# Expert blocks of two sizes, 512 and 256 rows, in place of 512 alone

## The chip, the cores and the metric

The kernel runs on one core of a Trainium2 chip. The metric is the device time of one execution in microseconds. The kernel before takes 2289.64 us, the median of three runs.

## What is computed

The input is 256 images of 128 channels and 7 x 7 pixels, that is 12544 tokens of 128 numbers. Six layers follow one another, each with a residual: window attention, attention over the pixels of an image with 1x1 convolutions, self-attention and a first mixture of experts, multi-scale self-attention and a second mixture of experts.

```python
def reference(x, ...):
    x = _L0_conv_ref(x, ...)
    x = _L1_conv_ref(x, ...)
    t = _to_tokens(x)
    t = t + _L2_attn_ref(_ln_t(t))
    t = t + _L2_ffn_ref(_ln_t(t), ...)
    t = t + _L3_attn_ref(_ln_t(t), ...)
    t = t + _L3_ffn_ref(_ln_t(t), ...)
    return _from_tokens(t, x)
```

Both mixtures have 8 experts, and each token goes to the two with the highest gate scores, so 25088 token-expert pairs (rows) are to be worked on in each. An expert is two matrix products with a Gelu between them, 128 to 192 to 128 numbers in the first mixture and 128 to 512 to 128 in the second:

```python
h = gelu(x @ W1[expert] + b1[expert])
y = h @ W2[expert] + b2[expert]
out = gate_1 * y_1 + gate_2 * y_2
```

## The kernel before

The program is a sequence of phases. The two that matter here are the expert stages, called moe2 and moe3 in names, and the dispatch phase ahead of each.

**Dispatch.** For each group of tokens it computes the two experts and gates, and GpSimd writes each token's row (128 numbers, and behind them its target row, its second expert and both gates; 528 bytes) to the region of its expert in `expert_rows`, in DRAM (L1558). Each expert has a region of its own of 13 x 1024 rows. When all are counted, `Dispatch.table` (L1512 to L1546, VectorE) turns the eight counts into a table of blocks: for each block its expert `blk_e`, its first row `blk_row` and the expert whose weights it takes, `blk_w`. A block is 512 rows of one expert; since a count need not be a multiple of 512, there are NBLK = 56 (L46), the most that any counts can need. Those left over point behind the last region, to a place without tokens. SyncE puts pad rows behind each expert's last token with eight stores (L1273). The constants of the table (`c_upto8`, `c_steps`, `c_blocks`) are loaded in `weights` (from L1250 on), ahead of `d_pad`, which holds the pad rows.

**Expert stage** (`blocks_phase`, from L2459 on). It runs the 56 blocks in order. Each weight and each row is kept as a high part in fp32r and the rest, so that a product takes three matmuls. The hidden layer is cut into K chunks: 2 of 96 for moe2, 4 of 128 for moe3. Each engine has an order of its own, written out by a loop over the chunks n of all blocks; the output of chunk n comes LAG = 2 behind its hidden part. Per block:

- SyncE loads 512 rows into `xb` (L2518) and one expert's weights into `w` (L2522), three buffers of each.
- TensorE turns the rows (4 transposes, L2533, `turn_x`), does three matmuls of 512 columns for each hidden chunk (L2545 to L2547) and three for each chunk's output (L2557 to L2559), and 4 transposes of the result (L2566, `turn_y`).
- ScalarE rounds the turned rows to `xh` (L2590), applies the Gelu (L2597), rounds every second chunk to `hh` (L2602), and adds the output bias (L2608).
- VectorE computes the low parts `xl` (L2627, `low_x`) and `hl` (L2638, `split`; L2636 rounds the other chunks), target rows and gates (`address`, L2649 to L2655), and multiplies the output with the gate into `yr` (L2661, `rows_y`).
- GpSimd scatters `yr` to `expert_out` by indirect DMA, 128 rows each, 4 a block (L2682).

`to` and `yr` have NY = 3 buffers. The wait in `address(b)` that keeps them whole is

```python
if b >= NY:
    dve.wait_ge(sent[j], 16 * S * (b // NY))
```

so VectorE waits there until the scatters of block b - 3 have landed. The order of VectorE's work in the program is

```python
for n in range(NBLK * K + LAG + 1):
    if n < NBLK * K:
        split(n)
        if n % K == K - 2:
            low_x(n // K + 1)
        if n % K == K - 1:
            address(n // K)
    if n >= LAG + 1 and (n - LAG - 1) % K == K - 1:
        rows_y((n - LAG - 1) // K)
```

## Time and profile before

| | |
|---|---|
| runs | 2283.72, 2291.57, 2289.64 us; median 2289.64 |
| profiled execution | 2285.74 us, span 2284.1 us |
| TensorE's mean granted clock | 0.891 of full speed |
| busy in the span | PE 1787.9 us, PEld 1236.1, DVE 1618.3, ACT 1404.3, POOL 1414.1 |
| scatters of moe2, first to last | 896.7 to 1201.5 us |
| scatters of moe3, first to last | 1820.8 to 2225.4 us |

PE is TensorE's matmuls, PEld its weight loads, DVE is VectorE, ACT ScalarE, POOL GpSimd, SP SyncE (SPq its queue of DMA issues). The span runs from the first to the last instruction; the execution's own time has 1.6 us more. Busy counts neither waits nor the issue of DMAs. The granted clock is the share of its full speed that TensorE was given, 1.00 being 2.4 GHz and 0.50 being 1.2 GHz.

### The profile page before, as it was taken

What the parts mean: (1) busy time and instruction counts of PE and PEld (TensorE: products, weight loads), DVE (VectorE), ACT (ScalarE), POOL (GpSimd) and SP (SyncE); (2) the same over time, 40 slices, a digit from 0 to 9 for tenths busy, and PEclk for the clock granted to TensorE, in tenths of its full rate; (3) what the DMA queues carried; (4) which work ended last, traced back from release to release, by engine and by line L of the source; (5) the groups of instructions that cost most, each with busy time, mean ns of one, the idle gap of its engine ahead of it and who ended that gap; (6) DMA issues with size and microseconds to landing.
All of it is one profiled execution on the core that took longest, in us unless ns stands there. A gap on an engine that the chain in (4) does not pass through costs nothing. (4 is left out here: it accounts for less than half of the span.)

```text
span 2284.1 us, 52612 instructions
## 1 busy us (share of the span) xinstructions
PE 1787.9 (78%) x16257; PEld 1236.1 (54%) x16257; DVE 1618.3 (71%) x4634; ACT 1404.3 (61%) x3208; POOL 1414.1 (62%) x1485
## 2 busy tenths in 40 slices
PE   7999997998777744777764777777786299999974
PEld 3555554776566643555543344444444177777763
DVE  5888887787677643666654588888786378888864
ACT  5777775564666523555540788888885267777750
POOL 3655554010177773777776378888888557767765
PEclk9999998999989857999985898998897599999995
DMA  6000000000221134666647012111110367777748
GB/s 116 17 0 0 0 0 2 1 0 18 74 83 55 55 89 124 185 180 179 174 122 249 9 60 68 55 56 55 60 36 30 98 222 232 227 231 234 226 131 338
DMA packets 169828, 233.57 MB, mean 102 GB/s; under 512 B 60032, under 2 KB 131957, under 8 KB 162190
## 3 DMA queue, kind: packets, MB, share of 16 engines
q1 hardware_dynamic: 142446, 172.32, 25.2%
q0 software_dynamic: 26880, 52.27, 6.8%
q10 hardware_dynamic: 288, 6.42, 0.7%
q8 instruction: 99, 1.62, 0.3%
q14 instruction: 115, 0.94, 0.1%
HBM read 155.37 MB, written 79.23 MB: 103 GB/s over the span
## 5 line engine op out<-in xcount | busy, mean ns | idle before, releaser
L2682 POOL DMA_INDIRECT expert_out<-moe_yr,moe_to x448 | 493.0, 1100 | 259.8 <-DVE moe_yr L2661 139.2
L1558 POOL DMA_INDIRECT expert_rows<-d_row,d_pos x392 | 380.8, 971 | 181.9 <-issue 164.8
L2597 ACT ACTIVATE moe_ah<-moe_hps,moe_w 128x512 f32<-128x512 f32 (+1 forms) x336 | 230.2, 685 | 204.3 <-PE moe_hps L2547 199.6
L2638 DVE TENSOR_TENSOR moe_hl<-moe_ah,moe_hh 128x512 fp32r<-128x512 f32 (+1 forms) x336 | 235.2, 700 | 95.6 <-ACT moe_hh L2602 89.3
L1775 PE MATMUL scales_ptps<-ident,scales_pr 113*128 113x113 f32 x512 | 104.2, 306 | 98.1 <-DVE scales_sc L1873 62.5
L550 POOL TENSOR_TENSOR window_pr<-window_pr,window_rc 113x392 f32<-113x392 f32 x128 | 108.9, 851 | 107.3 <-DVE window_rc L494 107.3
L2545 PE MATMUL moe_hps<-moe_xh,moe_w 128*128 128x512 f32 (+1 forms) x336 | 138.3, 412 | 35.5 <-DMA moe_w<-moe_split 31.4
L2533 PE MATMUL moe_xps<-ident,moe_xb 128*128 128x128 f32 x448 | 72.5, 286 | 102.6 <-DMA moe_xb<-expert_rows 102.6
L1775 PEld LDWEIGHTS scales_ptps<-ident,scales_pr 113*128 113x128 f32 x512 | 65.3, 157 | 152.3 <-DVE scales_sc L1873 68.7
L2557 PE MATMUL moe_yps<-moe_hh,moe_w 128*128 128x512 f32 (+1 forms) x336 | 144.3, 429 | 0.9 <-DVE moe_hl L2638 0.9
L538 POOL TENSOR_TENSOR window_sc<-window_sc,window_mx 113x392 f32<-113x392 f32 x128 | 107.8, 842 | 50.6 <-DVE window_mx L468 49.8
L2547 PE MATMUL moe_hps<-moe_xh,moe_w 128*128 128x512 f32 (+1 forms) x336 | 134.9, 401 | 0.0
L2546 PE MATMUL moe_hps<-moe_xl,moe_w 128*128 128x512 f32 (+1 forms) x336 | 134.5, 400 | 0.0
L2558 PE MATMUL moe_yps<-moe_hl,moe_w 128*128 128x512 f32 (+1 forms) x336 | 133.9, 398 | 0.0
L2559 PE MATMUL moe_yps<-moe_hh,moe_w 128*128 128x512 f32 (+1 forms) x336 | 133.3, 397 | 0.0
L2533 PEld LDWEIGHTS moe_xps<-ident,moe_xb 128*128 128x128 f32 x448 | 53.6, 144 | 134.2 <-DMA moe_xb<-expert_rows 125.3
L657 ACT ACTIVATE window_pt<-window_ptps 128x452 f32<-128x452 f32 x128 | 69.8, 545 | 90.9 <-PE window_ptps L334 90.8
L2004 POOL TENSOR_TENSOR scales_pr<-scales_pr,scales_fac 113x416 f32<-113x416 f32 x128 | 114.1, 903 | 2.7 <-DVE scales_fac L1911 1.3
L2627 DVE TENSOR_TENSOR moe_xl<-moe_xps,moe_xh 128x512 fp32r<-128x512 f32 x112 | 76.4, 682 | 54.6 <-ACT moe_xh L2590 54.6
L1071 POOL TENSOR_TENSOR conv_pr<-conv_pr,conv_rc 113x196 f32<-113x196 f32 x32 | 16.5, 516 | 154.4 <-DVE conv_rc L1037 154.4
L2602 ACT ACTIVATE moe_hh<-moe_ah 128x512 fp32r<-128x512 f32 (+1 forms) x168 | 106.2, 632 | 5.3
L2636 DVE CAST moe_hh<-moe_ah 128x512 fp32r<-128x512 f32 (+1 forms) x168 | 85.3, 508 | 27.1 <-ACT moe_ah L2597 27.1
(286 smaller groups left out, 5218.5 us busy)
## 6 DMA issues: line engine op xcount, KB each, us to landing
moe_w<-moe_split SPq DMA_DIRECT2D x56, 1026.5 KB
moe_xb<-expert_rows SPq DMA_DIRECT2D x112, 264.0 KB, 3.0
moe_w<-moe_split SPq DMA_DIRECT2D x56, 449.5 KB
c_yy<-expert_out SPq DMA_DIRECT2D x28, 448.0 KB, 7.1
final_yy<-expert_out SPq DMA_DIRECT2D x28, 448.0 KB, 7.7
expert_out<-moe_yr,moe_to POOLq DMA_INDIRECT x448
X<-in_x SPq DMA_DIRECT2D x32, 196.0 KB
expert_rows<-d_row,d_pos POOLq DMA_INDIRECT x392
```

The costliest lines, as they stand in the source:

```text
L1558: pool.indirect_dma_start(out=self.rows_dram, out_offset=bass.IndirectOffsetOnAxis(ap=self.pos[j][:, i, k:k + 1], axis=0), in_=self.row[j] ...
L1775: last = pe.transpose(ptps[:, hp * R:(hp + 1) * R], pr[at.r][p][:, 2 * hp:2 * hp + 2, :].rearrange("q h k -> q (h k)"), ident[0:R, 0:R])
L2533: last = pe.transpose(xps[:, t * C:(t + 1) * C], xb[b % NX][:, t, 0:C], ident[:, :])
L2545: pe.matmul(out, ww[:, W1H + k * P:W1H + (k + 1) * P], xh[j][:, :], start=True, stop=False)
L2546: pe.matmul(out, ww[:, W1H + k * P:W1H + (k + 1) * P], xl[j][:, :], start=False, stop=False)
L2547: pe.matmul(out, ww[:, W1L + k * P:W1L + (k + 1) * P], xh[j][:, :], start=False, stop=True).then_inc(h_mm, 1)
L2557: pe.matmul(out, ww[0:P, W2H + k * C:W2H + (k + 1) * C], high, start=(k == 0), stop=False)
L2558: pe.matmul(out, ww[0:P, W2H + k * C:W2H + (k + 1) * C], low, start=False, stop=False)
L2559: pe.matmul(out, ww[0:P, W2L + k * C:W2L + (k + 1) * C], high, start=False, stop=(k == K - 1)).then_inc(y_mm, 1)
L2597: act.activation(ah[n % NH][0:P, :], hps[n % 3][0:P, :], func, bias=bias(b, k)[0:P]).then_inc(h_done, 1)
L2638: dve.tensor_tensor(hl[n % NH][0:P, :], ah[n % NH][0:P, :], hh[n % NH][0:P, :].bitcast(F32), ALU.subtract).then_inc(hl_done, 1)
L2682: pool.indirect_dma_start(out=y_dram, out_offset=bass.IndirectOffsetOnAxis(ap=to[j][:, t:t + 1], axis=0), in_=yr[j][:, t, :], in_offset=No ...
```

## The change

The block of 512 rows stays, and a half block of 256 (PART) joins it. NBLK is 57: 48 full blocks (FULLS) and 9 half ones (HALVES). Halves are blocks 6, 12, 18, 25, 31, 37, 44, 50 and 56 (IS_HALF). An expert's rows are counted in units of 256; its pairs of units go to full blocks and the single one that may be left to a half, and where there are more pairs than full blocks, a pair goes to two halves. `rows(b)`, `tiles(b)` and `sent_until(b)` give a block's rows, its tiles of 128 and the scatters so far on its buffer. Everything that works on a block takes `rows(b)` columns: row load, transposes, matmuls, activations, VectorE's operations, and 2 scatters in place of 4. The weight load stays whole. The table of blocks takes 27 operations of VectorE in place of 15, with a table of marks of 512 numbers a partition (`c_marks`) in place of 64 (`c_upto8`), two sets of steps and three of block numbers.

```diff
-NBLK = (2 * TOKENS + EXPERTS * (BLOCK - 1)) // BLOCK
+PART = BLOCK // 2
+UNITS = (2 * TOKENS + EXPERTS * (PART - 1)) // PART
+FULLS = (UNITS - EXPERTS) // 2
+HALVES = UNITS - 2 * FULLS
+assert HALVES >= EXPERTS
+NBLK = FULLS + HALVES
+IS_HALF = [(b + 1) * HALVES // NBLK > b * HALVES // NBLK for b in range(NBLK)]
+ENDS = 2 * EXPERTS
...
-        self.upto8, self.steps, self.blocks = sb("upto8", [C, EXPERTS * EXPERTS]), sb("steps", [C, STEPS]), sb("blocks", [C, NBLK])
+        self.marks, self.steps, self.blocks = sb("marks", [C, 2 * ENDS * ENDS]), sb("steps", [C, 2 * STEPS]), sb("blocks", [C, 3 * NBLK])
...
-        self.past, self.gone = sb("past", [C, NBLK, EXPERTS]), sb("gone", [C, NBLK, EXPERTS])
+        self.past, self.gone = sb("past", [C, NBLK, ENDS]), sb("gone", [C, NBLK, ENDS])
...
+        dve.tensor_scalar(pairs[:, :], as_pair, all_pairs, None, ALU.is_lt).then_inc(tab, 1)
...
+        dve.wait_ge(tab, 15)
+        dve.tensor_tensor(self.past[:, :, :], begun[:, :][:, :, None].to_broadcast(per_block),
+                          ends[:, 0:ENDS][:, None, :].to_broadcast(per_block), ALU.is_ge).then_inc(tab, 1)
+        dve.wait_ge(tab, 16)
+        dve.tensor_tensor(self.gone[:, :, :], self.past[:, :, :], ends[:, ENDS:2 * ENDS][:, None, :].to_broadcast(per_block),
+                          ALU.mult).then_inc(tab, 1)
         dve.tensor_reduce(sh.blk_e[:, :], self.past[:, :, :], AX_X, ALU.add).then_inc(tab, 1)
-        dve.tensor_tensor(self.gone[:, :, :], self.past[:, :, :], full[:, :][:, None, :].to_broadcast(per_block), ALU.mult).then_inc(tab, 1)
-        dve.wait_ge(tab, 9)
-        dve.tensor_reduce(begun[:, :], self.gone[:, :, :], AX_X, ALU.add).then_inc(tab, 1)
-        dve.wait_ge(tab, 10)
-        dve.tensor_tensor(begun[:, :], self.blocks[:, :], begun[:, :], ALU.subtract).then_inc(tab, 1)
-        dve.tensor_scalar(where[:, :], sh.blk_e[:, :], float(REGION), None, ALU.mult).then_inc(tab, 1)
-        dve.wait_ge(tab, 12)
-        dve.scalar_tensor_tensor(out=where[:, :], in0=begun[:, :], scalar=float(BLOCK), in1=where[:, :], op0=ALU.mult,
+        dve.tensor_tensor(begun[:, :], place, pairs[:, :], ALU.mult).then_inc(tab, 1)
+        dve.wait_ge(tab, 19)
+        dve.tensor_reduce(where[:, :], self.gone[:, :, :], AX_X, ALU.add).then_inc(tab, 1)
+        dve.scalar_tensor_tensor(out=sh.blk_e[:, :], in0=pairs[:, :], scalar=float(EXPERTS), in1=sh.blk_e[:, :], op0=ALU.mult,
                                  op1=ALU.add).then_inc(tab, 1)
-        dve.wait_ge(tab, 13)
+        dve.wait_ge(tab, 21)
+        dve.tensor_scalar(sh.blk_e[:, :], sh.blk_e[:, :], float(EXPERTS), None, ALU.subtract).then_inc(tab, 1)
+        dve.tensor_tensor(where[:, :], where[:, :], begun[:, :], ALU.add).then_inc(tab, 1)
+        dve.wait_ge(tab, 23)
+        dve.tensor_scalar(where[:, :], where[:, :], float(BLOCK), None, ALU.mult).then_inc(tab, 1)
+        dve.tensor_scalar(sh.blk_w[:, :], sh.blk_e[:, :], float(EXPERTS - 1), None, ALU.min).then_inc(tab, 1)
+        dve.wait_ge(tab, 25)
+        dve.scalar_tensor_tensor(out=where[:, :], in0=sh.blk_e[:, :], scalar=float(REGION), in1=where[:, :], op0=ALU.mult,
+                                 op1=ALU.add).then_inc(tab, 1)
...
+    def rows(b):
+        return PART if IS_HALF[b] else BLOCK
+
+    def tiles(b):
+        return rows(b) // C
+
+    def sent_until(b):
+
+        return sum(tiles(i) for i in range(b % NY, b, NY))
...
-                sp.dma_start(xb[b % NX][:, :, :], rows_dram[bass.ds(r, BLOCK)].rearrange("(t p) c -> p t c", p=C)).then_inc(x_loaded[b % NX], 16)
+                sp.dma_start(xb[b % NX][:, 0:tiles(b), :], rows_dram[bass.ds(r, rows(b))].rearrange("(t p) c -> p t c", p=C)).then_inc(x_loaded[b % NX], 16)
...
-                out = hps[n % 3][0:P, :]
-                pe.matmul(out, ww[:, W1H + k * P:W1H + (k + 1) * P], xh[j][:, :], start=True, stop=False)
-                pe.matmul(out, ww[:, W1H + k * P:W1H + (k + 1) * P], xl[j][:, :], start=False, stop=False)
-                pe.matmul(out, ww[:, W1L + k * P:W1L + (k + 1) * P], xh[j][:, :], start=False, stop=True).then_inc(h_mm, 1)
+                out = hps[n % 3][0:P, 0:n_rows]
+                pe.matmul(out, ww[:, W1H + k * P:W1H + (k + 1) * P], xh[j][:, 0:n_rows], start=True, stop=False)
+                pe.matmul(out, ww[:, W1H + k * P:W1H + (k + 1) * P], xl[j][:, 0:n_rows], start=False, stop=False)
+                pe.matmul(out, ww[:, W1L + k * P:W1L + (k + 1) * P], xh[j][:, 0:n_rows], start=False, stop=True).then_inc(h_mm, 1)
...
-                act.activation(ah[n % NH][0:P, :], hps[n % 3][0:P, :], func, bias=bias(b, k)[0:P]).then_inc(h_done, 1)
+                act.activation(ah[n % NH][0:P, 0:n_rows], hps[n % 3][0:P, 0:n_rows], func, bias=bias(b, k)[0:P]).then_inc(h_done, 1)
...
-                    dve.wait_ge(sent[j], 16 * S * (b // NY))
+                    dve.wait_ge(sent[j], 16 * sent_until(b))
...
-                for t in range(S):
+                for t in range(tiles(b)):
                     pool.indirect_dma_start(out=y_dram, out_offset=bass.IndirectOffsetOnAxis(ap=to[j][:, t:t + 1], axis=0),
```

The other matmuls, transposes, copies and subtractions are narrowed in the same way as those shown. On GpSimd each expert stage has 210 scatters where it had 224.

VectorE in moe2 from the address of block 8 to the gated rows of block 7, right behind the half block 6 (`second`, `gate` and `to` are of `address`, `hh` and `hl` of `split`, `xl` is `low_x`, `yr` is `rows_y`). Before, from the same place:

```order
L2649 TENSOR_SCALAR moe2_second<-moe2_xb2,blk_e 128x4
L2651 TENSOR_TENSOR moe2_gate2<-moe2_second,moe2_xb2 128x4
L2652 SCALAR_TENSOR_TENSOR moe2_to2<-moe2_second,moe2_xb2 128x4
L2655 TENSOR_TENSOR moe2_gate2<-moe2_xb2,moe2_gate2 128x4
L2636 CAST moe2_hh2<-moe2_ah2 96x512
L2638 TENSOR_TENSOR moe2_hl2<-moe2_ah2,moe2_hh2 96x512
L2627 TENSOR_TENSOR moe2_xl0<-moe2_xps,moe2_xh0 128x512
L2661 TENSOR_TENSOR moe2_yr1<-moe2_tps1,moe2_gate1 128x512
```

Now:

```order
L2699 TENSOR_SCALAR moe2_second<-moe2_xb2,blk_e 128x4
L2701 TENSOR_TENSOR moe2_gate2<-moe2_second,moe2_xb2 128x4
L2702 SCALAR_TENSOR_TENSOR moe2_to2<-moe2_second,moe2_xb2 128x4
L2705 TENSOR_TENSOR moe2_gate2<-moe2_xb2,moe2_gate2 128x4
L2686 CAST moe2_hh2<-moe2_ah2 96x512
L2688 TENSOR_TENSOR moe2_hl2<-moe2_ah2,moe2_hh2 96x512
L2676 TENSOR_TENSOR moe2_xl0<-moe2_xps,moe2_xh0 128x512
L2711 TENSOR_TENSOR moe2_yr1<-moe2_tps1,moe2_gate1 128x512
```

Nothing moved here, and every row is as wide as it was: the operations between the wait for block 5's scatters and the rows for GpSimd are all of full blocks. Those of the half block itself stand ahead of it, among them:

```order
L2711 TENSOR_TENSOR moe2_yr1<-moe2_tps0,moe2_gate1 128x512
L2688 TENSOR_TENSOR moe2_hl1<-moe2_ah1,moe2_hh1 96x256
L2699 TENSOR_SCALAR moe2_second<-moe2_xb0,blk_e 128x2
L2701 TENSOR_TENSOR moe2_gate0<-moe2_second,moe2_xb0 128x2
L2702 SCALAR_TENSOR_TENSOR moe2_to0<-moe2_second,moe2_xb0 128x2
L2705 TENSOR_TENSOR moe2_gate0<-moe2_xb0,moe2_gate0 128x2
L2686 CAST moe2_hh2<-moe2_ah2 96x512
L2688 TENSOR_TENSOR moe2_hl2<-moe2_ah2,moe2_hh2 96x512
```

`yr1` is block 4's, at full width, and `hl1`, `second`, `gate0` and `to0` are block 6's, 256 columns and 2 tiles wide.

VectorE in moe3, from the last split of block 6 to the split of block 7's third chunk and `low_x` of block 8. Before:

```order
L2638 TENSOR_TENSOR moe3_hl3<-moe3_ah3,moe3_hh3 128x512
L2649 TENSOR_SCALAR moe3_second<-moe3_xb0,blk_e 128x4
L2651 TENSOR_TENSOR moe3_gate0<-moe3_second,moe3_xb0 128x4
L2652 SCALAR_TENSOR_TENSOR moe3_to0<-moe3_second,moe3_xb0 128x4
L2655 TENSOR_TENSOR moe3_gate0<-moe3_xb0,moe3_gate0 128x4
L2636 CAST moe3_hh0<-moe3_ah0 128x512
L2638 TENSOR_TENSOR moe3_hl0<-moe3_ah0,moe3_hh0 128x512
L2638 TENSOR_TENSOR moe3_hl1<-moe3_ah1,moe3_hh1 128x512
L2636 CAST moe3_hh2<-moe3_ah2 128x512
L2638 TENSOR_TENSOR moe3_hl2<-moe3_ah2,moe3_hh2 128x512
L2627 TENSOR_TENSOR moe3_xl0<-moe3_xps,moe3_xh0 128x512
```

Now:

```order
L2688 TENSOR_TENSOR moe3_hl3<-moe3_ah3,moe3_hh3 128x256
L2699 TENSOR_SCALAR moe3_second<-moe3_xb0,blk_e 128x2
L2701 TENSOR_TENSOR moe3_gate0<-moe3_second,moe3_xb0 128x2
L2702 SCALAR_TENSOR_TENSOR moe3_to0<-moe3_second,moe3_xb0 128x2
L2705 TENSOR_TENSOR moe3_gate0<-moe3_xb0,moe3_gate0 128x2
L2686 CAST moe3_hh0<-moe3_ah0 128x512
L2688 TENSOR_TENSOR moe3_hl0<-moe3_ah0,moe3_hh0 128x512
L2688 TENSOR_TENSOR moe3_hl1<-moe3_ah1,moe3_hh1 128x512
L2686 CAST moe3_hh2<-moe3_ah2 128x512
L2688 TENSOR_TENSOR moe3_hl2<-moe3_ah2,moe3_hh2 128x512
L2676 TENSOR_TENSOR moe3_xl0<-moe3_xps,moe3_xh0 128x512
```

The split and `address` of block 6 are half as wide; block 7's splits and `low_x` of block 8, which come before TensorE can start block 8, are not.

The table of blocks on VectorE, its middle part, as it is now:

```order
L1559 TENSOR_TENSOR d2_begun<-d2_begun,d2_apart 128x57
L1561 TENSOR_TENSOR d2_past<-d2_begun,d2_ends 128x912
L1564 TENSOR_TENSOR d2_gone<-d2_past,d2_ends 128x912
L1566 TENSOR_REDUCE blk_e<-d2_past 128x57
L1567 TENSOR_TENSOR d2_begun<-d2_blocks,d2_pairs 128x57
L1569 TENSOR_REDUCE d2_where<-d2_gone 128x57
L1570 SCALAR_TENSOR_TENSOR blk_e<-d2_pairs,blk_e 128x57
L1573 TENSOR_SCALAR blk_e<-blk_e 128x57
L1574 TENSOR_TENSOR d2_where<-d2_where,d2_begun 128x57
```

`past` and `gone` have 912 elements a partition (57 x 16) where they had 448 (56 x 8).

## Rows read from the trace of the kernel before

**Rows 1.** Windows view, the two expert stages of core 0 (busy us per engine).

```profile
core 0: us, PE busy (x) PEld busy (x) DVE busy (x) ACT busy (x) POOL busy (x), PEclk, DMA share, GB/s
896.70:1201.50 304.80, 223.60 (x1070) 155.48 (x1070) 191.11 (x483) 165.74 (x267) 224.88 (x224) 0.96 0.59 168
1837.00:2205.00 368.00, 357.90 (x1719) 285.20 (x1718) 295.98 (x647) 266.60 (x429) 254.61 (x212) 1.00 0.72 226
```

**Rows 2.** Waits, 895 to 1170: line, releaser, us waited, times, longest.

```profile
DVE moe_second L2649 <- DMA expert_out<-moe_yr,moe_to: 52.1, 41, 3.1
```

**Rows 3.** Timeline, moe2, VectorE and GpSimd: start, us, operation, [wait before <- releaser].

```profile
949.22 0.68 DVE L2661 TENSOR_TENSOR moe_yr<-moe_tps,moe_gate 128x512 f32<-128x512 f32 x1
...
950.67 0.98 POOL L2682 DMA_INDIRECT expert_out<-moe_yr,moe_to  x1 [0.88 <-DVE moe_yr L2661]
...
1100.52 0.98 POOL L2682 DMA_INDIRECT expert_out<-moe_yr,moe_to  x1 [0.30 <-issue]
...
1102.92 0.23 DVE L2649 TENSOR_SCALAR moe_second<-moe_xb,blk_e 128x4 f32<-128x4 f32 x1 [1.16 <-DMA expert_out<-moe_yr,moe_to]
...
1105.13 0.68 DVE L2661 TENSOR_TENSOR moe_yr<-moe_tps,moe_gate 128x512 f32<-128x512 f32 x1
```

**Rows 4.** Timeline, moe3: SyncE's loads and the first wait for weights.

```profile
1822.02 0.37 SPq L2522 DMA_DIRECT2D moe_w<-moe_split  x1
...
1827.93 0.28 PEld L2545 LDWEIGHTS moe_hps<-moe_xh,moe_w 128*128 128x128 f32 x1 [3.69 <-DMA moe_w<-moe_split]
...
1845.21 0.38 SPq L2518 DMA_DIRECT2D moe_xb<-expert_rows  x1
...
2195.07 0.38 SPq L2518 DMA_DIRECT2D moe_xb<-expert_rows  x1
```

**Rows 5.** Timeline, moe3: one block's beginnings on TensorE, SyncE and VectorE.

```profile
1991.44 0.35 SPq L2522 DMA_DIRECT2D moe_w<-moe_split  x1
...
1991.76 0.40 PE L2545 MATMUL moe_hps<-moe_xh,moe_w 128*128 128x512 f32 x1
1991.77 0.19 PEld L2546 LDWEIGHTS moe_hps<-moe_xl,moe_w 128*128 128x128 f32 x1
...
1993.15 0.40 PE L2545 MATMUL moe_hps<-moe_xh,moe_w 128*128 128x512 f32 x1
...
2000.02 0.39 PE L2545 MATMUL moe_hps<-moe_xh,moe_w 128*128 128x512 f32 x1
...
2001.00 0.69 DVE L2638 TENSOR_TENSOR moe_hl<-moe_ah,moe_hh 128x512 fp32r<-128x512 f32 x1 [0.66 <-ACT moe_hh L2602]
```

**Rows 6.** Windows view, five short stretches of moe2: one, and the sum.

```profile
1059.00:1062.40 3.40, 3.40 (x12) 2.66 (x11) 1.58 (x7) 0.60 (x2) 2.65 (x3) 0.50 0.46 170
...
sum 16.60, PE 16.60 PEld 12.93 DVE 11.84 ACT 3.69 POOL 11.40; mean PE 3.32 PEld 2.59 DVE 2.37 ACT 0.74 POOL 2.28
```

**Rows 7.** Timeline, first dispatch: TensorE's weight loads for matmuls of 8 columns.

```profile
658.97 0.97 PEld L1313 LDWEIGHTS d_small<-d_wgc,X 128*128 128x128 f32 x8
```

**Rows 8.** Groups by form: line, engine, operation, xcount, busy us, mean ns, idle before.

```profile
L2597 ACT ACTIVATE moe_ah<-moe_hps,moe_w 128x512 f32<-128x512 f32 x224 | 153.9, 687 | 106.9 <-PE moe_hps L2547 104.7
...
L2112 ACT ACTIVATE scales_ef<-scales_low 113x256 f32<-113x256 f32 x32 | 13.3, 415 | 0.0
...
L1024 DVE TENSOR_TENSOR conv_sc<-conv_sps,conv_mx 113x196 f32<-113x196 f32 x32 | 11.6, 362 | 1.1
```

**Rows 9.** Timeline, end of moe3: the last block's first matmul, the last scatter.

```profile
2205.79 0.40 PE L2545 MATMUL moe_hps<-moe_xh,moe_w 128*128 128x512 f32 x1
...
2224.46 0.98 POOL L2682 DMA_INDIRECT expert_out<-moe_yr,moe_to  x1 [0.30 <-issue]
```

**Rows 10.** Timeline, second dispatch: the table of blocks and the pad stores.

```profile
1798.37 0.17 DVE L1517 COPY d_total<-scales_sorted 128x8 f32<-128x8 f32 x1
...
1799.51 9.37 SPq L1273 DMA_DIRECT2D expert_rows<-d_pad  x8
...
1799.95 0.62 DVE L1530 TENSOR_TENSOR d_past<-d_blocks,d_ends 128x448 f32<-128x448 f32 x1
...
1803.16 0.18 DVE L1545 TENSOR_SCALAR blk_w<-blk_e 128x56 int32<-128x56 f32 x1
```

More of the change, by code:

```diff
@@ L1513, in table @@
         sh, tab = self.sh, self.tab
-        per_block = [C, NBLK, EXPERTS]
-        total, full, ends, begun, where = self.total, self.full, self.ends, self.begun, self.where
+        wide, per_block = [C, 2, EXPERTS, STEPS], [C, NBLK, ENDS]
+        total, units, ends, pairs, apart, begun, where = self.total, self.units, self.ends, self.pairs, self.apart, self.begun, self.where
+        as_pair, as_single, place = [self.blocks[:, k * NBLK:(k + 1) * NBLK] for k in range(3)]
+        all_pairs = ends[:, EXPERTS - 1:EXPERTS]
         dve.wait_ge(self.total_mm, 1)
@@ L2685, in _ @@
             for j in range(NY):
-                pool.wait_ge(sent[j], 16 * S * len(range(j, NBLK, NY)))
+                pool.wait_ge(sent[j], 16 * sum(tiles(b) for b in range(j, NBLK, NY)))
 def combine_phase(nc, sh, kind, y_dram, loads):
```

101 lines of the change are left out of this document (65 added, 36 removed).

## The prediction

> **What bounds the kernel now.** I read first where the two expert stages lie and how busy each engine is in them [rows 1]; then in each stage who waits and for whom; then one block's period, instruction by instruction. The change touches the rest of the program only in the table of blocks.
>
> *First expert stage (moe2, two chunks a block): GpSimd.* Its 224 scatters take the 304.8 us of [rows 1], and it is busy for 224.9 of them. The 0.30 us between two scatters with no releaser named is its own issue, so a scatter costs 0.98 + 0.30 = about 1.29 us from start to start, 5.16 us a block, 289 us for 56; the other 16 us are longer scatters and short waits. VectorE waits 52.1 us, 41 times, for scatters to land [rows 2]: that is `address(b)`, which may not overwrite the addresses of block b-3 before they are sent. This makes a loop, to be followed in [rows 3]: the last scatter of one block ends at 1100.52 + 0.98 = 1101.50; `address` of the block three later starts at 1102.92, 1.42 on; then VectorE runs without a gap through `address`, a cast, a subtraction, `low_x` and `rows_y` until 1105.81, 2.89 later. Where GpSimd waits for `rows_y`, it starts 0.77 after its end (949.22 + 0.68 = 949.90, then 950.67). So from the end of block b-3's scatters to the first scatter of block b-1 at least 1.42 + 2.89 + 0.77 = 5.08 us pass. GpSimd itself, with block b-2 between, needs 0.30 + 4.82 + 0.30 = 5.42. The loop is hidden by 0.34 us. That is the number that matters for this stage.
>
> *Second stage (moe3, four chunks a block): TensorE.* Block periods are exactly regular: the row loads go out at 1845.21 and 2195.07, 51 blocks apart, 6.86 us a block [rows 4], at granted clock 1.00 and with TensorE busy 357.9 of 368.0 us [rows 1]. Six matmuls of 512 columns, three of a hidden chunk and three of an output, lie between 1991.76 and 1993.15, so one takes 0.23 us from start to start, 24 of them 5.5 us, 8 transposes 0.9, and 0.4 are short waits [rows 5].
>
> **The change, part by part.** Rows worked on fall from 56 x 512 = 28672 to 48 x 512 + 9 x 256 = 26880, that is by 3.5 full blocks a stage; blocks rise from 56 to 57. Taken straight through this would be worth 3.5 x 5.16 = 18 us and 3.5 x 6.86 = 24 us. I don't expect both.
>
> *moe2.* Put a half block H in the place of b-2 in the loop above. GpSimd now needs 0.30 + (0.98 + 1.29) + 0.30 = 2.87 us between its neighbours, but the loop still takes 5.08, since everything VectorE does in it (`address` of H+2, first chunk of H+3, `low_x`, `rows_y` of H+1) belongs to full blocks. GpSimd waits 2.2 us after every half, and a half block saves only 5.42 - 5.08 = 0.34 us against a full one. The sum of pure issue: 48 x 5.16 + 8 x 4.82 + 2.6 (the last half has nothing behind it) = 288.9, against 289.0: nothing, for 14 fewer scatters. What may come on top: TensorE is idle in the new waits, and it is already the clock's prey here. [Rows 6] show one of five short stretches (begun at about 1059, 1114, 1138, 1148, 1172) at granted clock 0.50; GpSimd was busy for only 11.4 of their 16.6 us together. If all of the 16 us of waste are theirs, one costs 3.2 us. With a half TensorE has 12 x 0.117 + 4 x 0.11 = 1.8 us of work in a place of 4.8 us. I take two more such stretches at half of that price: +3 us. Bounds for the stage: -18 (the loop gives way, all of the 14 scatters are won) and +26 (a stretch at 3.2 us after each of eight halves).
>
> *moe3, one half matmul.* No fp32r matmul of 256 columns is in the trace. Half of 0.231 is 0.116; the floor by the weight load is in [rows 7]: eight loads of 128 columns, with matmuls of only 8 columns behind them, go by in 0.97 us; the last takes 0.19 (the load in [rows 5]), so one starts each 0.111 us. The load is thus just covered, and I take 0.117. If load and stream came one after the other it would be 0.111 + 0.107 = 0.22, nearly the price of a full one. In [rows 5] they don't: the load for L2546 starts at 1991.77 while the matmul of L2545 has just begun (1991.76). The Trainium skill says otherwise (TensorE: Matmul & The Clock Gate, part 3, section "The mechanism": a weight load overlaps matmuls in flight only when its row group differs); all of these use all 128 rows, and by that rule a half would bring TensorE nothing. It is a rival below.
>
> *moe3, the half block.* TensorE alone would need 6.86 - 24 x (0.231 - 0.117) - 4 x 0.11 = 3.7 us. But the other engines' halves cost more than half: by the nearest sizes of [rows 8] a VectorE operation falls from 0.69 to about 0.42, a ScalarE one from 0.69 to about 0.45. With T the start of H's first matmul, VectorE's order from [rows 5] gives: last split of H-1 done at T + 1.67 (2001.00 + 0.69 - 2000.02; TensorE is there at T + 1.39 and waits), then `address` of H-1, the splits of H's chunks 0 to 2, `low_x` of H+1 at full size, done T + 4.9. H+1's first matmul can start at T + 5.0, not 3.7. In H+1's window the outputs of H's last two chunks are short and TensorE catches up to 6.1 us, so the two windows take 11.1 us for 13.7, and 0.2 are saved in the window before (a shorter `turn_x`): H costs 4.1 us. Bounds: 3.7 and 5.0. The last block's first matmul comes 55 x 6.86 = 377.3 us after the first one's now (2205.79 [rows 9]), then 48 x 6.86 + 8 x 4.1 = 362.1: 15.2 earlier. From there to the end of the last scatter it is now 2224.46 + 0.98 - 2205.79 = 19.65 us; with a half, scatters of block 55 start at T + 5.7 (`rows_y` ends T + 4.9), six of them, done at T + 13.4. That is 6.2 earlier; I leave some for what a tail loses between its steps, and call it 5 us. Stage: -20; bounds -13 and -25.
>
> Weights are loaded once more in each stage, a full one for a half block. In moe3 a load goes out (1991.44) 1.7 us before the next block's first matmul (1993.15) and is needed a whole block after that [rows 5]: 8.6 us later, with H between 1.7 + 5.0 = 6.7. The first load took 1827.93 - 1822.02 = 5.9 with two others beside it [rows 4]: covered.
>
> *Table.* 15 operations of 5.0 us (1798.37 to 1803.34) become 27. From 0.18 (56 elements) and 0.62 (448) [rows 10] an operation costs 0.12 + 1.12 us a thousand elements, so the four of 57 x 16 = 912 take 1.1 each and the whole about 10.6. In the second dispatch it then ends at 1798.4 + 10.6 = 1809.0, while the pad stores issue until 1808.9 and have still to land: hidden, just; were the cover gone, 5.6 a stage. The first dispatch has the same operations beside the same stores. The mark table makes 256 KB of 32: it is loaded ahead of `d_pad`, which starts both stages; at the 226 GB/s of [rows 1] the 224 KB more take 1.0 us at most. I put +0.7 for both.
>
> **Sum:** -20 + 3 - 0.2 + 0.7 = -16.5 us, on the profiled execution's 2285.7: 2269.2. That execution lies 3.9 under the median of three and inside their spread of 7.8, so I name 2270.
>
> **The rivals.**
> 1. *GpSimd keeps its pace in moe2.* For it: the loop is hidden now, `rows_y` is mostly early by half a microsecond. Against: 0.34 us is all the room there is. Time: 2285.7 - 20 - 18 + 0.7 = 2248.
> 2. *Slower: the clock.* After each half TensorE has a thin stretch, and falls to 0.50. It costs 3.2 us a time in moe2 by the above and, in moe3, where TensorE is the bound, half of a stretch as long as those of [rows 6], 1.7. Without stretches the sum stands at -19.5; six in moe2 use it up, that is the point from which it decides; eight in each stage make 2285.7 - 19.5 + 26 + 14 = 2306. For it: five falls in 56 full blocks. Against: in moe3 the clock is 1.00 for 368 us and H's window stays filled with work of H-1 and H+1; in moe2 the wait gives the blocks behind it a microsecond of room. [...]
> 3. *The skill's weight rule holds.* H costs 6.86 - 24 x 0.01 - 0.44 = 6.2 us in moe3; 48 x 6.86 + 8 x 6.2 = 378.9, 1.6 later, tail 4 shorter: 2285.7 - 2.4 + 3 + 0.7 = 2287, no change.
> 4. *The table or the loads come onto the path:* 11 us at most, 2280.
>
> **How the numbers follow.** My forecast has a chance of 0.66, rival 1 0.13, rival 2 0.11, rival 3 0.04, rival 4 0.06. 0.3% is 7 us, about what this measurement can tell. The range 2253 to 2284 holds the forecast with its bounds, rival 4 and part of rivals 1 and 2. Faster: 0.83 (the forecast, rivals 1 and 4 nearly whole); same 0.09; slower 0.08.
>
> **What would show it.** In moe2 the scatters fall to 210, but the span from first to last stays within a few us of 304.8; after each of blocks 6, 12, 18, 25, 31, 37, 44, 50 GpSimd waits about 2.2 us for `rows_y` of the next block, and VectorE's wait for `address` there is gone. In moe3 256-column matmuls stand 0.115 to 0.125 us apart, clock stays 1.00, TensorE's waits in a half's window are for `moe_hl` and `moe_xl`, and first to last row load shrinks by about 15 us. I am wrong if moe2 shrinks by over 8 us, if a half in moe3 costs over 5 us, or if ScalarE or a weight load, not VectorE, holds it.

## The result and the profile after

The changed kernel takes 2304.02 us, the median of 4 runs (2299.46 to 2307.04), against 2289.21 of the kernel before in the same comparison: a ratio of 1.007, with a 95% interval of 1.0046 to 1.0094. It is slower. The time lies outside my range of 2253 to 2284, on the side to which I had given 0.08. A later comparison with more runs (12 and 35) gives 1.0026, interval 1.0008 to 1.0045: still slower, by 6 us and not by 15. The two intervals do not quite meet, so the sign of the loss is shown and its size is known only as 2 to 22 us.

The profiled execution takes 2307.04 us, its span is 2305.3, that is 21.2 more than before. I cut both spans at the same instructions. The third column is a second profile of the same changed kernel (after_again, below). (1820.8 us, where the table of times before lets moe3's scatters begin, is its first row load; its first scatter starts at 1843.3.)

| stage, us | before | changed | changed again |
|---|---|---|---|
| start to the first row load of moe2 | 877.9 | 882.0 | 877.1 |
| to moe2's first scatter | 18.8 | 19.3 | 19.1 |
| moe2, first to last scatter | 304.8 | 305.2 | 315.6 |
| **from there to the next phase** | **2.9** | **10.6** | **10.6** |
| combine and multi-scale attention, to the table | 594.0 | 608.3 | 600.8 |
| table to the first row load of moe3 | 22.5 | 22.0 | 23.1 |
| to moe3's first scatter | 22.5 | 22.1 | 22.0 |
| moe3, first to last scatter | 382.1 | 369.0 | 367.3 |
| **from there to the next phase** | **2.9** | **10.6** | **10.6** |
| the rest | 55.7 | 56.2 | 55.7 |

moe2 stood still as forecast and moe3 gave 13 to 15 us. (The 315.6 of the second profile is no loss: four profiles with the changed moe2 stage, 210 scatters and three buffers, gave 304.6, 305.2, 312.9 and 315.6 us, three with 224 scatters and three buffers 304.8, 313.4 and 314.7.) What took them back stands in the two bold rows, 7.7 us each: a place that I had not looked at. There the engines meet at the end of a phase. Ahead of the meeting GpSimd executes a drain, an instruction of its sequencer, and those are not in the engine's busy time. The view of one source line shows it (engine, operation, count, min/median/max ns, first and last start in us). Before:

```profile
L2468 POOLq DRAIN  x2: 702/702/702, 1202.8 to 2226.8; - x2
```

And in the changed kernel:

```profile
L2516 POOLq DRAIN  x2: 8379/8379/8379, 1207.9 to 2239.8; - x2
```

In the timeline it is only a hole between GpSimd's last scatter and SyncE's first load of the combine phase, 11.6 us from start to start, to be compared with before's 3.85 (1200.49 to 1204.34):

```profile
1205.48 0.98 POOL L2732 DMA_INDIRECT expert_out<-moe_yr,moe_to  x1 [0.30 <-issue]
1217.06 2.31 SPq L2767 DMA_DIRECT2D c_yy<-expert_out  x5
```

**moe2 and moe3 in the windows view**, to be held against [rows 1]: GpSimd's busy time fell by 11.1 us in moe2 and the stage didn't; in moe3 the clock stayed at 1.00.

```profile
901.30:1206.50 305.20, 217.12 (x1054) 154.36 (x1052) 184.61 (x492) 159.36 (x272) 213.83 (x210) 0.93 0.58 165
1863.00:2222.00 359.00, 342.47 (x1708) 272.69 (x1706) 280.64 (x652) 256.94 (x436) 226.42 (x198) 1.00 0.73 230
```

The loop of [rows 3] behind the first half block, in the timeline (block 6 is the half; these are its second scatter, the address of block 8, the gated rows of block 7, the first scatter of block 7 and the address of block 9):

```profile
936.80 0.23 DVE L2699 TENSOR_SCALAR moe_second<-moe_xb,blk_e 128x4 f32<-128x4 f32 x1 [0.62 <-DMA expert_out<-moe_yr,moe_to]
...
937.36 0.99 POOL L2732 DMA_INDIRECT expert_out<-moe_yr,moe_to  x1 [0.32 <-issue]
...
939.06 0.68 DVE L2711 TENSOR_TENSOR moe_yr<-moe_tps,moe_gate 128x512 f32<-128x512 f32 x1
940.51 1.35 POOL L2732 DMA_INDIRECT expert_out<-moe_yr,moe_to  x1 [2.17 <-DVE moe_yr L2711]
940.92 0.22 DVE L2699 TENSOR_SCALAR moe_second<-moe_xb,blk_e 128x4 f32<-128x4 f32 x1
```

GpSimd waits 2.17 us for the gated rows, where I had written 2.2, and the wait of block 9's address is gone, as forecast. Behind the other seven halves that have a block after them the wait was 2.4 to 3.0 us, and 2.4 to 4.3 behind the eight of the second profile.

**A half block of moe3**, TensorE's first matmuls of blocks 6 (the half), 7 and 8, to be held against [rows 5]:

```profile
1895.84 0.28 PE L2593 MATMUL moe_hps<-moe_xh,moe_w 128*128 128x256 f32 x1
1895.95 0.28 PE L2594 MATMUL moe_hps<-moe_xl,moe_w 128*128 128x256 f32 x1
...
1901.12 0.47 PE L2593 MATMUL moe_hps<-moe_xh,moe_w 128*128 128x512 f32 x1
...
1907.69 0.50 PE L2593 MATMUL moe_hps<-moe_xh,moe_w 128*128 128x512 f32 x1 [0.25 <-DMA moe_w<-moe_split]
```

Matmuls of 256 columns follow each other by 0.11 to 0.12 us. The two windows take 11.85 us, where I had 11.1: 0.3 more for the half, and 0.5 more for the second, in which stands a wait for a weight load that I had called covered.

**The table of blocks**, in the timeline, to be held against [rows 10]:

```profile
1825.37 0.17 DVE L1531 COPY d_total<-scales_sorted 128x8 f32<-128x8 f32 x1
...
1826.86 9.26 SPq L1281 DMA_DIRECT2D expert_rows<-d_pad  x8
...
1830.31 1.11 DVE L1561 TENSOR_TENSOR d_past<-d_begun,d_ends 128x912 f32<-128x912 f32 x1
...
1835.92 0.19 DVE L1582 TENSOR_SCALAR blk_row<-d_where 128x57 int32<-128x57 f32 x1
```

It takes 10.7 us (forecast 10.6) and ends 0.01 us ahead of the last pad store's issue.

### The profile page after: what moved, and what is told of

Same layout as the page of the kernel before. It is cut to its first block and busy times, and to the rows that moved or that the text cites. A ratio compares the mean times of both kernels' runs of the same rounds, so it can differ in the third digit from the quotient of the medians.

```text
span 2305.3 us, 52637 instructions
## 1 busy us (share of the span) xinstructions
PE 1784.7 (77%) x16237; PEld 1235.0 (54%) x16237; DVE 1608.3 (70%) x4679; ACT 1387.8 (60%) x3221; POOL 1376.3 (60%) x1457
## 5 line engine op out<-in xcount | busy, mean ns | idle before, releaser
L2732 POOL DMA_INDIRECT expert_out<-moe_yr,moe_to x420 | 452.7, 1078 | 286.2 <-DVE moe_yr L2711 177.5
L2646 ACT ACTIVATE moe_ah<-moe_hps,moe_w 128x512 f32<-128x512 f32 (+3 forms) x342 | 222.8, 652 | 201.0 <-PE moe_hps L2595 197.7
L2688 DVE TENSOR_TENSOR moe_hl<-moe_ah,moe_hh 128x512 fp32r<-128x512 f32 (+3 forms) x342 | 223.4, 655 | 102.3 <-ACT moe_hh L2651 96.0
L2593 PE MATMUL moe_hps<-moe_xh,moe_w 128*128 128x512 f32 (+3 forms) x342 | 136.6, 399 | 43.8 <-DMA moe_w<-moe_split 37.5
L2605 PE MATMUL moe_yps<-moe_hh,moe_w 128*128 128x512 f32 (+3 forms) x342 | 142.3, 416 | 2.4 <-DVE moe_hl L2688 2.3
L2594 PE MATMUL moe_hps<-moe_xl,moe_w 128*128 128x512 f32 (+3 forms) x342 | 131.0, 383 | 0.0
L2606 PE MATMUL moe_yps<-moe_hl,moe_w 128*128 128x512 f32 (+3 forms) x342 | 131.0, 383 | 0.0
L2607 PE MATMUL moe_yps<-moe_hh,moe_w 128*128 128x512 f32 (+3 forms) x342 | 130.8, 382 | 0.0
L2595 PE MATMUL moe_hps<-moe_xh,moe_w 128*128 128x512 f32 (+3 forms) x342 | 130.7, 382 | 0.0
L2651 ACT ACTIVATE moe_hh<-moe_ah 128x512 fp32r<-128x512 f32 (+3 forms) x171 | 102.2, 598 | 5.4
L2593 PEld LDWEIGHTS moe_hps<-moe_xh,moe_w 128*128 128x128 f32 (+1 forms) x342 | 62.8, 184 | 78.7 <-DMA moe_w<-moe_split 57.8
L2676 DVE TENSOR_TENSOR moe_xl<-moe_xps,moe_xh 128x512 fp32r<-128x512 f32 (+1 forms) x114 | 73.0, 640 | 45.7 <-ACT moe_xh L2638 45.7
```

Of the source, the lines that this page charges most:

```text
L2593: pe.matmul(out, ww[:, W1H + k * P:W1H + (k + 1) * P], xh[j][:, 0:n_rows], start=True, stop=False)
L2594: pe.matmul(out, ww[:, W1H + k * P:W1H + (k + 1) * P], xl[j][:, 0:n_rows], start=False, stop=False)
L2595: pe.matmul(out, ww[:, W1L + k * P:W1L + (k + 1) * P], xh[j][:, 0:n_rows], start=False, stop=True).then_inc(h_mm, 1)
L2605: pe.matmul(out, ww[0:P, W2H + k * C:W2H + (k + 1) * C], high, start=(k == 0), stop=False)
L2606: pe.matmul(out, ww[0:P, W2H + k * C:W2H + (k + 1) * C], low, start=False, stop=False)
L2607: pe.matmul(out, ww[0:P, W2L + k * C:W2L + (k + 1) * C], high, start=False, stop=(k == K - 1)).then_inc(y_mm, 1)
```

## The experiments

Ratios are against the kernel before on the same chip, with their 95% intervals; a single run has none, and only its trace is read. Two theories on the drain stood first: it waits for rows that were scattered a short time ago (R), or it goes by the number of scatters (C); and two on the attention stage, whose code is the same in both kernels and which grew by 13 us: by chance of the clock (A), or through the change (B).

**after_again.** No edit.

> The changed kernel once more, nothing edited. Of the 21.3 us between the two profiled executions, 13.2 lie in the multi-scale attention (502.6 us before, 515.8 after, from its first GpSimd product to the table of blocks), whose code is the same in both; its granted clock was 0.87 and 0.81. Theory A (the clock there varies from one execution to the next and has nothing to do with the change): this profile gives another length, 503 to 516, with the clock moving along. Theory B (the change fixes it): 515 to 517 at 0.81 again. The drain of GpSimd behind the last scatter of each expert stage should be 8.4 us twice, as in the first profile of this kernel, by every theory.

2299.39 us, ratio 1.0026 (1.0008 to 1.0045). From its first GpSimd product to the table, the attention stage took 507.6 us, after 502.6 in the first profile of before and 515.8 in that of the change. Over six profiles of the kernel before and its variants it lay between 502.6 and 511.9, over eleven of the changed one and its variants between 503.7 and 515.9, longest where the granted clock was lowest (0.81). The changed kernel's stage isn't fixed at 515 to 517, so theory B as it stood falls and most of the 13 us are chance. That none of it is the change's isn't shown: both profiles over 512 us are of changed kernels, and the means are 506.3 and 508.6. Both drains were 8.38 us again.

**real_rows_last.**

```diff
-    one["c_blocks"] = np.tile(np.arange(NBLK, dtype=f), (C, 1))
+    one["c_blocks"] = np.tile(np.arange(NBLK, dtype=f)[::-1], (C, 1))
```

> The kernel before, 56 blocks of 512 and 224 scatters a stage, with the block numbers of the table counted down: the three empty blocks come first and a block with real rows last. Nothing else differs. Theory R: GpSimd's drain behind each stage takes 8.4 us instead of 0.7, the kernel is 15 us slower (2304), which is the whole loss of the change. Theory C (count of scatters): drain 0.7, time unchanged at 2289.

2294.47 us, ratio 1.0006 (0.9992 to 1.002), drains as before:

```profile
L2468 POOLq DRAIN  x2: 702/702/702, 1213.6 to 2245.3; - x2
```

The empty blocks now come first, and the drain is as short as before: R falls.

**halves_last.**

```diff
-IS_HALF = [(b + 1) * HALVES // NBLK > b * HALVES // NBLK for b in range(NBLK)]
+IS_HALF = [b >= FULLS for b in range(NBLK)]
```

> The nine half blocks stand at the end of each stage, the 48 full ones ahead. With this input four of the nine are empty in moe2 and three in moe3, so that the stage ends with 8 and 6 scatters that write nothing, 10 and 8 us long. Theory R (GpSimd's drain waits for real rows that were scattered a short time ago): the drain falls from 8.4 us to between 0.7 and 3 in both stages. Theory C (the drain depends on how many scatters the stage had; 210 as in the changed kernel): it stays at 8.4. In moe2 the loop over VectorE is then not met by a half among full ones: first to last scatter 287 us instead of 305 (14 scatters of 1.29 us fewer). In moe3 a half block among halves is bound by its weight load, 4.5 to 5.9 us each; stage within 3 us of the changed kernel's. In sum 25 to 32 us under the changed kernel by R, 13 to 18 under it by C.

2286.83 us, ratio 0.9979 (0.9963 to 0.9996). The drains stay at 8.38, so C holds against R once more. moe2 takes 295.1 us, 8 more than I said, but 10 less than with the halves spread; moe3 366.0. A half among halves costs 4.1 to 5.9 us from row load to row load.

**four_buffers.**

```diff
-    NW, NX, NH, NY = 3, 3, 4, 3
+    NW, NX, NH, NY = 3, 3, 4, 4
```

> The changed kernel with four buffers of addresses and gated rows instead of three. My theory of moe2 is that after each half block GpSimd waits 2.2 us because VectorE may not write the addresses of block b before the scatters of block b-3 have landed. Then a fourth buffer takes that wait away: first to last scatter 305 us falls to 287 to 292, and the waits of 2.2 to 2.9 us after blocks 6, 12, 18 go to 0.3. Rival: VectorE or TensorE is late there for another reason (the clock); then the stage stays at 303 to 306. The drains stay at 8.4 us, and moe3 stays.

2286.85 us, ratio 0.9978 (0.9962 to 0.9995). moe2 takes 293.7 us, just above the 287 to 292 that I expected. All waits of VectorE ahead of `address` are gone (53.1 us for scatters and 7.7 without a releaser in the changed kernel, none here). GpSimd's waits for the gated rows, from the view of waits (us in total, times, longest; the longest lies ahead of the first scatter), first in the changed kernel, then here:

```profile
POOL expert_out L2732 <- DVE moe_yr L2711: 58.9, 27, 30.1
```

```profile
POOL expert_out L2732 <- DVE moe_yr L2711: 49.9, 18, 30.5
```

**before_four_buffers.** The same edit in the kernel before.

> The kernel before with four buffers of addresses and gated rows instead of three. Theory: the loop over VectorE is hidden by 0.34 us behind a full block in between, and shows only after a half one or after a disturbance, so that here the stage of 304.8 us loses 0 to 5. Rival: the loop binds all along, with and without halves; then this kernel gains as much in moe2 as the changed one did, 11 us and more, and the half blocks have nothing to do with it. The drain stays at 0.7 us (224 scatters); should it be 8.7, then it follows from the number of buffers.

2284.4 us, ratio 0.997 (0.9955 to 0.9985); moe2 298.4 us. Here the same row reads 35.4, 14, 29.8, where it was 41.6, 16, 29.6. So the loop costs 6 us without halves, and 9 to 12 with them: it was not fully hidden in the kernel before either. The drain was 1.36 us.

**count_208_209.** Scatters stop at a total; what is left out writes nothing with this input.

```diff
+            total = {"moe2": 208, "moe3": 209}[kind]
...
-                for t in range(tiles(b)):
+                for t in range(max(0, min(tiles(b), total - sum(tiles(i) for i in range(b))))):
```

> The changed kernel without the last scatters of each stage: 208 in moe2 and 209 in moe3 instead of 210 (the last block has no rows there with this input; what it leaves out is the scatter of an empty block). So far GpSimd's drain took 0.70 us behind 224 scatters, 8.38 behind 210, 7.57 and 7.73 behind the 196 of the dispatches; real rows or empty ones at the end made no difference. Theory C16 (GpSimd makes up a last batch of 16, so the drain is short where the count is a multiple of 16 and grows with what is missing): 0.7 behind 208, and 8.7 to 8.9 behind 209. Theory D (long whenever the count is not 224, or the length depends on something else in the code, such as the half blocks): 8.4 behind both. 32 in place of 16 would give about 3 to 9 behind 208, but not 0.7.

```profile
L2516 POOLq DRAIN  x2: 8216/8256/8297, 1208.8 to 2238.4; - x2
```

8.22 us behind 208, 8.30 behind 209. The multiple of 16 is refuted; each scatter adds 0.08. The single run took 2305.31 us.

**count_216_220.** The same in the kernel before, with 216 and 220.

> The kernel before without the last scatters of each stage (of empty blocks): 216 in moe2 and 220 in moe3 instead of 224. Theory C16, with 0.81/2 = 0.4 us for each one missing, from 8.38 (14 missing) and 7.57 (12 missing): 8 missing give about 6.0, 4 missing about 4.3. If the cost was in proportion alone (0.55 each) it would be 5.1 and 2.9. Theory D (the half blocks make the drain long): 0.7 in both, since this kernel has none.

```profile
L2468 POOLq DRAIN  x2: 8869/9032/9196, 1194.4 to 2221.7; - x2
```

This is the kernel before, without any half block, and its drain is 8.87 and 9.20 us. So the half blocks have nothing to do with it. The first stage ended 10 us sooner for 8 scatters fewer, and gave 8.2 back in the drain; the kernel took 2289.59 in its single run.

**count_232_240.** The kernel before with scatters added that write nothing (a tile of target rows out of bounds).

```diff
+            pool.memset(far[:, :], int(FAR)).then_inc(far_set, 1)
+            pool.wait_ge(far_set, 1)
...
...
+                for _ in range(((1 if 8 <= b < 16 else 0) * (2 if kind == 'moe3' else 1)) if kind in ('moe2', 'moe3') else 0):
+                    n_pad += 1
+                    pool.indirect_dma_start(out=y_dram, out_offset=bass.IndirectOffsetOnAxis(ap=far[:, 0:1], axis=0),
+                                            in_=sh.ident[:, :], in_offset=None, bounds_check=2 * TOKENS - 1,
+                                            oob_is_err=False).then_inc(padding, 16)
```

> The kernel before with empty scatters added, 8 in moe2 and 16 in moe3, so that the stages have 232 and 240. If the drain falls once, between 220 and 224, and then rises again at 0.08 us for each scatter, it is 0.7 to 2 behind 232 and 1.4 to 3 behind 240. If 224 is special (a multiple of 32), it is back at 9 to 10 us behind 232 and 240.

```profile
L2468 POOLq DRAIN  x2: 4296/4296/4296, 1219.1 to 2258.7; - x2
```

Neither expectation: 4.30 us behind both. The single run took 2321.15 us.

**changed_padded.** The changed kernel with 14 such scatters in moe3, so that this stage has 224.

```diff
+                for _ in range((1 if 8 <= b < 22 else 0) if kind in ('moe3',) else 0):
...
```

> The changed kernel with one addition: 14 empty scatters in moe3, blocks 8 to 21, where GpSimd has time; 224 scatters there. If the long drain is the part that turned the gain of moe3 into a loss, the drain there falls from 8.38 to 0.7 to 1.2, moe3 keeps its 367 to 369 us, and the kernel is 7 us faster than the changed one, level with the kernel before within 0.2%. Rival: the drain's length falls but the barrier behind it comes no earlier, or the extra scatters lengthen moe3; then nothing is gained.

2290.64 us, ratio 0.9999 (0.9984 to 1.0014). The row shows moe3's drain as the smaller, moe2's as the larger:

```profile
L2516 POOLq DRAIN  x2: 1846/5112/8379, 1205.6 to 2228.0; - x2
```

moe3 still took 367.2 us; the phase behind came 4.0 us after the last scatter, for 10.6. Fourteen scatters more take the ratio from 1.0026 to 0.9999: without the long drain in one stage the loss is gone.

**last_four_padded.** The edits of halves_last, four_buffers and changed_padded together.

> Half blocks at the end, four buffers of addresses and gated rows, and in moe3, where GpSimd has time, 14 more scatters that write nothing (blocks 8 to 21), so that this stage has 224. By C16 the drain behind moe3 is 0.7 us, behind moe2 it stays at 8.7. moe2 first to last scatter: 287 us if the fourth buffer and the place of the halves add up, 293 if either alone gives all there is. moe3 stays at 366, as the extra scatters fit into GpSimd's waits of 1.1 us a block and its room of 1.7. In sum against the kernel before 18 to 24 us: 2269 to 2275. By D the drain behind moe3 stays long and it is 8 less.

2266.11 us (5 runs), ratio 0.9886 (0.986 to 0.9912): the best kernel of the study, faster than both. Drains 8.71 and 1.19 us; moe2 292.9, moe3 366.7.

**evenly_four_padded.** The edits of four_buffers and changed_padded together, halves evenly placed.

> As the best version, but with the half blocks evenly placed as the change has them: four buffers, 14 empty scatters in moe3. Tells what the place of the halves is worth when the loop over VectorE does not bind: moe2 293 to 295 and moe3 367 to 368, that is within 2 us of the version with the halves last. Drains 8.7 and 1.2. 2267 to 2274 in all.

2279.65 us, ratio 0.9962 (0.9944 to 0.9979). I expected the place to be worth at most 2 us; the medians differ by 13.5, the profiles by 6.6 in moe2 and 2.3 in moe3. The drain behind moe3 was 2.01. Between after_again and halves_last the place was worth 12.6 us of medians too. Why it counts when VectorE's wait is gone I can't show. In moe2 the gaps between GpSimd's scatters sum up to 84.6 us here and 80.1 with the halves last, and the scatters themselves to 214.9 and 212.8; that is where the 6.6 us lie, and not their cause.

**small_pads.** last_four_padded, and 14 scatters of 16 rows in moe2.

```diff
+            n_pad, few = 0, 16 if kind == "moe2" else C
...
```

> The best version so far (half blocks last, four buffers, 14 empty scatters in moe3) with 14 empty scatters of 16 rows each in moe2 too, blocks 8 to 21, so that both stages have 224. The drains so far: 7.57 and 7.73 behind 196, 8.22 behind 208, 8.30 (209), 8.38 (210), 8.87 (216), 9.20 (220), 0.70 behind 224; the multiple of 16 is refuted by 208. Theory I (scatter instructions are counted, whatever their rows): drain 0.7 to 1.4 behind moe2, and small scatters cost GpSimd less than the 1.29 us of a full one. Theory J (rows are counted): 224 instructions but 27104 rows of 28672, drain 8.5 to 9. Time of moe2: at 1.29 us a pad, 293 + 18 less what falls into waits; if the price goes with the rows, 295. Against the kernel before: 2262 to 2266 with I and cheap pads, 2276 to 2280 with I and dear ones, 2270 to 2285 with J.

2273.13 us (6 runs), ratio 0.993 (0.991 to 0.995). Both drains are 1.19 us, so instructions are counted and not rows. But a scatter of 16 rows takes 0.86 us of GpSimd where one of 128 takes 0.98:

```profile
945.20 0.86 POOL L2741 DMA_INDIRECT expert_out<-ident,moe_far  x1 [0.30 <-issue]
```

Fourteen of them are 16.2 us of GpSimd with their issue. moe2 grew by 6.6 of that, from 292.9 to 299.5, since the gaps between scatters fell from 80.1 to 74.7 us, and the drain fell by 7.5. So in the profiles the pads of moe2 are worth nothing, and by the medians they cost 7 us; which of the two holds isn't shown.

**spare_memsets, late_drain, drain_midway** ask what the drain is. The edits are, in this order:

```diff
+                if 8 <= b < 22:
+                    pool.memset(spare[:, 0:16], 0.0).then_inc(spared, 1)
+                    pool.wait_ge(spared, b - 7)
```

```diff
+            for i in range(24):
+                pool.memset(spare[:, :], 0.0).then_inc(spared, 1)
+                pool.wait_ge(spared, i + 1)
```

```diff
+                if b == 28:
+                    pool.drain()
```

> The kernel before, 224 scatters a stage, with 14 small memsets on GpSimd in each stage (blocks 8 to 21). Theory S (the drain's length goes by the scatters that GpSimd has issued): 0.70 us, as before. Theory I (it goes by the length or place of GpSimd's program, which the number of scatters also changes): it changes, to somewhere between 1 and 9 us.

> The changed kernel with 24 memsets of 512 numbers a partition on GpSimd behind the last wait for the scatters, so that some 10 to 20 us pass between the last scatter's landing and the drain. Theory T (what the drain waits for goes on by itself, 8 us after the scatters): the drain falls to 0.7. Theory W (the drain does work of its own, by the count of scatters): it stays at 8.4, and the stage ends 8.4 us after the memsets.

> The changed kernel with one more drain on GpSimd ahead of block 28's scatters in each stage (102 scatters by then, 108 after it). Theory W: the work is done in two parts, so the drain at the end is shorter than 8.38, by 0.08 us for each of the 102 scatters, that is 8.4 - 8.3 = about 0.1 to 0.7; or, if its length goes by the count since the program's start, it stays. Theory T: both drains take as long as it takes from the last scatter, 8 us each, whatever the count.

Their drains in the same order, with drain_midway's extra drain as the last row (single runs of 2295.51, 2333.3 and 2312.92 us, beside one of the kernel before of 2299.78):

```profile
L2468 POOLq DRAIN  x2: 702/702/702, 1211.8 to 2237.2; - x2
```

```profile
L2516 POOLq DRAIN  x2: 8374/8376/8379, 1228.0 to 2266.0; - x2
```

```profile
L2516 POOLq DRAIN  x2: 8704/8704/8704, 1213.8 to 2244.3; - x2
...
L2732 POOLq DRAIN  x2: 8542/8542/8542, 1051.0 to 2052.5; - x2
```

More instructions on GpSimd don't change it. 14 us between the last scatter's landing and the drain don't shorten it: it isn't a wait for something outside GpSimd that finishes by itself (GpSimd itself was busy with the memsets). And a drain after 102 scatters costs 8.54 us, and the one at the end, 108 scatters later, still 8.70.

**What the kept traces show between the scatters.** This was read in them afterwards, and no run was made to test it. Between two scatters of an expert stage GpSimd takes 0.30 us where it waits for nothing. In all 25 stages without added scatters or an extra drain the gap ahead of scatter 114 is longer, 0.9 to 2.2 us, and names no releaser. The last such gap of a stage stands ahead of scatter 222 of 224 in moe3 of the kernel before:

```profile
2221.89 0.98 POOL L2682 DMA_INDIRECT expert_out<-moe_yr,moe_to  x1 [2.16 <-issue]
```

ahead of scatter 114 of 210 in moe3 of the changed kernel:

```profile
2071.03 1.22 POOL L2732 DMA_INDIRECT expert_out<-moe_yr,moe_to  x1 [2.16 <-issue]
```

and ahead of scatters 186 of 232 and 194 of 240 in count_232_240:

```profile
1152.27 1.33 POOL L2686 DMA_INDIRECT expert_out<-moe_yr,moe_to  x1 [2.16 <-issue]
...
2182.40 1.16 POOL L2686 DMA_INDIRECT expert_out<-moe_yr,moe_to  x1 [1.69 <-issue]
```

Counted from the last such gap, the drains fall into order:

| scatters behind the gap | 3 | 9 | 47 | 95 | 96 | 97 | 103 | 107 |
|---|---|---|---|---|---|---|---|---|
| stage's scatters | 224 | 224 | 232, 240 | 208 | 209 | 210 | 216 | 220 |
| drain, us | 0.70 | 1.19 | 4.30 | 8.22 | 8.30 | 8.38 | 8.87 | 9.20 |

That is 0.46 us and 0.082 for each scatter, within 0.01 for all of them. (The 9 are moe3 of last_four_padded and small_pads.) With four buffers it was otherwise 0.33 more: 8.71 behind 97, and 1.36 behind 7 in moe3 of before_four_buffers. In drain_midway the gap ahead of scatter 114 is only 0.30: the extra drain took its place, and the drain at the end stands for the 108 scatters since. Two things keep this from being a rule. Seven stages with a short drain show no gap near their end: moe2 of the kernel before, real_rows_last, spare_memsets, before_four_buffers and small_pads, and moe3 of changed_padded and evenly_four_padded. And a few gaps of 1.0 to 1.4 us without a releaser stand where the count does not start again, as ahead of scatter 161 of moe3 in both profiles of the changed kernel (1.2 us).

## Why the prediction was wrong

**The step that failed** is one that I did not write. I followed the stage up to "the end of the last scatter" and took what comes after as fixed. That term stands at nothing in my sum, without a reason. It was 2.9 us and became 10.6, twice: +15.4 us, 7.7 of drain in each. None of my rivals has it; rival 2 was on the right side by another mechanism. The rows before could have warned me. The same drain takes 7.57 and 7.73 us behind the 196 scatters of either dispatch:

```profile
L2189 POOLq DRAIN  x1: 7570/7570/7570, 868.6 to 868.6; - x1
```

```profile
L1592 POOLq DRAIN  x1: 7730/7730/7730, 1811.2 to 1811.2; - x1
```

and only 0.70 behind the expert stages. That 224 scatters end three behind a gap, with a short drain, was luck that the kernel before had; 210 end 97 behind one and lost it.

**moe2 (+2.8 with everything).** The mechanism was right: the wait of 2.2 us after each half, VectorE's wait gone, no gain for 14 fewer scatters (304.8 to 305.2). GpSimd's waits for gated rows went from 41.6 to 58.9 us, 17 more, about what 14 scatters of 1.29 us save. Rival 1 needed that pace kept and is refuted here; a fourth buffer brings part of it (293.7).

**moe3 (-20).** Half was right. The matmul of 256 columns at 0.117 us, VectorE as the one that holds the next block, and the tail (2224.81 to 2237.48 + 0.98 is 13.65 us for 19.65, 6.0 less where I had 5) came out. The term that was mis-sized is the half block: the last block's first matmul came 370.2 us after the first one's (1854.57 to 2224.81) for 377.9 before, 7.6 earlier and not 15.2; first to last row load shrank by 7.5 us, not 15. At 6.86 for each of 48 full blocks, a half costs 5.1 us and not 4.1, over the 5 that I had called wrong; that a weight load has a part in it was another such sign. In the windows above 0.3 of the difference is the half itself and 0.5 the window with the wait for the weights of the block two later: I had set 6.7 us of room against 5.9 of a load at the stage's start, and here it went out at 1900.22 and the matmul that waited for it started 7.5 us later, at 1907.69. Once, at block 19, right behind the half block 18, that wait was 2.02 us (the first row; the second is TensorE's waits for weights in the whole stage, us in total, times, longest; before it had none):

```profile
1987.86 0.50 PE L2593 MATMUL moe_hps<-moe_xh,moe_w 128*128 128x512 f32 x1 [2.02 <-DMA moe_w<-moe_split]
```

```profile
PE moe_hps L2593 <- DMA moe_w<-moe_split: 2.8, 3, 2.0
```

So a weight load for half the rows is not covered everywhere. Stage -13 to -15, at my lower bound.

**Table and loads (+0.7).** 10.7 us and hidden in the second dispatch. From the second table's start to the first row load it took 22.0 to 23.1 us for 22.5, so nothing that can be seen; from the first one's 34.0 and 33.9 for 33.0 (848.03 to 882.00 and 843.07 to 876.99, for 844.86 to 877.88), where the change may have cost 1 us.

**The weight rule (rival 3).** Load and stream one after the other would have made a 256-column matmul 0.22 us. In the rows above they start 0.11 to 0.12 us apart, each with a weight load of its own and on all 128 rows, and rival 3 is out. The Trainium skill (TensorE: Matmul & The Clock Gate, part 3, section "The mechanism") has the rule that a weight load overlaps matmuls in flight only when its row group differs; the trace disagrees with it.

**The clock (rival 2).** In moe3 it was 1.00 as forecast. In moe2 it was 0.93 and 0.89 in the two profiles, for 0.96 and 0.92 in two of the before kind, so the halves may cost TensorE some clock. But a stretch at the low clock behind each half would have made moe2 26 us longer, and over the profiles of both kinds it wasn't longer at all.

**The sum**, by the profiles: drains +15.4, moe3 -14, moe2 and the table between 0 and +2. That makes 1 to 3 us of loss, beside an attention stage that was 2.3 us longer in the mean of the changed kinds, which may be chance. The 6 us of the larger comparison (interval 2 to 10) fit this; the 15 of the first, with 4 runs of either kernel, are not accounted for.

**What stays open:** what GpSimd does in the drain and in the gap ahead of scatter 114, why a gap of 2 us ends a count that a drain of 8 us ends too, and why some stages show no gap. Shown is that the drain goes by scatters and not by rows, place, time or length of program.
